# Three stages of a fused block in one program block, with the token lists written during the middle one

## The reference

```python
x = x + xattn(_layernorm(x), ctx)      # q, k, v, o with LoRA; 257 context rows and the own 32 keys
x = x + rwkv_moe(_layernorm(x), ...)   # below
x = x + ffn(_layernorm(x), ...)        # shared GEGLU + one of 8 experts by argmax

# rwkv_moe
xn = _ln(x, ln1_g, ln1_b); xx = _shift(xn)
k, v, r = xk @ Wk, xv @ Wv, sigmoid(xr @ Wr)     # xk = xn*mu + xx*(1-mu), and so on
wkv = scan over the positions of exp-weighted sums of v
x = x + r * wkv @ Wo
ei = _ln(x, ln2_g, ln2_b); exx = _shift(ei)
probs = softmax(ei @ router_w); vals, idx = top_k(probs, 2)
k_e = square(relu(xk_e @ eWk[e])); r_e = sigmoid(xr_e @ eWr[e])
moe = sum over the two experts of weight * r_e * (k_e @ eWv[e])
return x + moe
```

## Time and profile before

| | us |
|---|---|
| median of three runs | 1025.69 (1024.75 to 1028.22) |
| the profiled execution | 1025.3 |
| its span, first to last instruction | 1023.6 |
| DVE in 157 to 304 (time mixing) | 120.5 of 147 busy |
| PE in 304 to 348 (routing) | 3.2 of 44 busy |
| PE in 348 to 542 (first experts) | 191.4 of 194 busy |

### The profile page before, as it was taken

How to read it: one execution, slowest core, us unless ns; L and a number is a source line. 1 busy time by engine, 2 the same in 40 slices (tenths; PEclk the granted TensorE clock), 3 DMA queues, 4 the chain that set the end, 5 groups by cost and what they waited for, 6 DMA issues and landing times. The chain is left out here.

```text
span 1023.6 us, 19906 instructions
## 1 busy us (share of the span) xinstructions
PE 893.4 (87%) x6694; PEld 809.5 (79%) x6695; DVE 438.7 (43%) x1126; ACT 291.2 (28%) x648; POOL 279.8 (27%) x520
## 2 busy tenths in 40 slices
PE   6899987889850499999995999995899999999995
PEld 4566657888840399999994999995799999999994
DVE  2354445999956455555552333335211111111113
ACT  1333324666620254554441111110011111111110
POOL 1664442444443232232203222220210010010006
PEclk8999998999965599999997999997999999999998
DMA  9887828511110242222212111010588988899715
GB/s 348 290 291 276 303 83 285 147 42 32 33 39 4 93 161 86 80 79 87 77 51 63 32 42 37 31 31 27 196 315 331 321 300 327 305 317 326 276 58 164
DMA packets 97918, 163.40 MB, mean 160 GB/s; under 512 B 10136, under 2 KB 76184, under 8 KB 95672
## 3 DMA queue, kind: packets, MB, share of 16 engines
q1 hardware_dynamic: 85552, 120.84, 34.4%
q0 software_dynamic: 6528, 19.54, 7.0%
q10 hardware_dynamic: 5776, 22.22, 5.4%
HBM read 146.06 MB, written 16.52 MB: 159 GB/s over the span
## 5 line engine op out<-in xcount | busy, mean ns | idle before, releaser
L1306 PEld LDWEIGHTS bank<-zT_f,we 128*128 128x128 f32 x1472 | 167.8, 192 | 3.3 <-issue 1.5
L1306 PE MATMUL bank<-zT_f,we 128*128 128x128 f32 x1472 | 168.3, 275 | 1.6 <-issue 1.1
L1323 DVE TENSOR_TENSOR hT_f<-bank,act_g 128x512 f32<-128x512 f32 x78 | 53.8, 691 | 230.4 <-PE bank L1306 217.1
L1315 ACT ACTIVATE act_g<-bank 128x512 f32<-128x512 f32 x78 | 46.6, 597 | 323.7 <-PE bank L1306 323.7
L1306 PE MATMUL bank<-zT_c,a_x 128*128 128x128 f32 x1024 | 122.7, 283 | 0.3 <-PEq L978 0.3
L1306 PEld LDWEIGHTS bank<-zT_c,a_x 128*128 128x128 f32 x1024 | 120.5, 199 | 0.8 <-issue 0.7
L726 PE MATMUL bank<-xn,mixed_w 128*128 128x128 f32 x768 | 94.0, 280 | 1.3 <-ACT xn L808 0.9
L726 PEld LDWEIGHTS bank<-xn,mixed_w 128*128 128x128 f32 x768 | 90.0, 195 | 2.3 <-ACT xn L808 1.3
L1330 PE MATMUL bank<-we,hT_f 128*128 128x256 f32 x368 | 83.3, 380 | 0.0
L1183 PE MATMUL bank<-xk,wk_e 128*128 128x128 f32 x624 | 78.0, 280 | 0.2
L1183 PEld LDWEIGHTS bank<-xk,wk_e 128*128 128x128 f32 x624 | 74.5, 196 | 0.9 <-DVE xr L1237 0.5
(11 more groups left out here) (227 smaller groups left out, 1286.7 us busy)
## 6 DMA issues: line engine op xcount, KB each, us to landing
we<-in_W_dram SPq DMA_DIRECT2D x69, 1024.0 KB, 7.3
ctx_sb<-in_ctx_n_dram ACTq DMA_DIRECT2D x16, 1152.0 KB, 7.4
kT<-in_ctx_t_dram SPq DMA_DIRECT2D x16, 1028.0 KB, 8.9
rows_y<-y SPq DMA_DIRECT2D x39, 128.0 KB, 1.7
ewk_sb<-in_eWk_dram SPq DMA_DIRECT2D x1, 4096.0 KB, 14.2
ewv_sb<-in_eWv_dram SPq DMA_DIRECT2D x1, 4096.0 KB
rows_f<-yr ACTq DMA_DIRECT2D x23, 128.0 KB, 6.2
ewr_sb<-in_eWr_dram SPq DMA_DIRECT2D x1, 2048.0 KB, 19.8
```

Of the source, the lines that this page charges most:

```text
L1306: last = nc.tensor.matmul(bank[half][:, f * P:(f + 1) * P], w12[:, i, k, col0:col0 + P], zT[:, k], start=k == 0, stop=k == KD - 1)
L1315: nc.scalar.activation(act_g[:, half], bU[half][:], ACT.Gelu).then_inc(self.ac_g, 1)
L1323: nc.vector.tensor_tensor(hT[:, parity, half * HH:(half + 1) * HH].rearrange("p f t -> p (f t)"), bG[half][:], act_g[:, half], ALU.mult).t ...
```

## The change

Attention, time mixing and first experts become one block; the routing block between them is gone. The semaphores of all three are cleared once, behind the experts.

- **Joint.** Each engine's list has attention steps 15, 16, 17 alternating with steps 0, 1, 2 of time mixing (`MIX_AT`), then steps 3 to 21. Buffers of the stages share two arenas; the expert weights are loaded when the last `x1` is written (`dv_x1`).
- **Step of time mixing.** DVE no longer adds the logits; for chunk s-5 it finds the two best experts (`largest`, `largest_at`), the one-hot rows, their sum (`mask`), the rank of the token in the expert and a row of a list (`listed`). The sum of weights goes to PSUM (`bB`), `key_rise` is one instruction. PE adds the router's bias by a product and makes the ranks by two products (`ranks`); ACT copies the logits (`router`). POOL orders its pairs by semaphores in place of drains, adds the mask to the running count (`count`), and last in its step, for chunk s-6, writes the token numbers to `tab_e` in DRAM by two indirect stores of 128 single elements (`list_tokens`).
- **Behind the last chunk** DVE makes the map of the 39 tiles (`tile_map`). SP then reads, for each tile, the place of its list from SBUF and loads 128 token numbers (`load_pick`), nine tiles ahead. POOL's loop over the tiles is written out: mix factors, gather, and for 16 tiles a piece of the addition of `a_x2` to `x1`.
- The mix factors `cm_mu` come with another load.

The core of the diff:

```diff
-            nc.clear_and_free_semaphores(att_sems)
-            nc.all_engine_barrier()
...
-            nc.clear_and_free_semaphores(mix_sems)
-            nc.all_engine_barrier()
...
-        routing("r1_", 2, NT1, logits, True, table1, expert1, slot1, gate, add_x2)
...
+        MIX_AT = G - 1
+        ATT_STEPS = G + 2
+        MIX_STEPS = G + 6
...
+            @block.vector
+            def _(dve):
+                att, mix = att_vector(dve), mix_vector(dve)
+                for s in range(ATT_STEPS):
+                    att(s)
+                    if s >= MIX_AT:
+                        mix(s - MIX_AT)
+                for s in range(ATT_STEPS - MIX_AT, MIX_STEPS):
+                    mix(s)
+                moe_vector(dve)
...
+            def list_tokens(n):
+                if n == 0:
+                    pool.wait_ge(zero_tab_out, 16)
+                pool.wait_ge(dv_slot, n + 1)
+                for k in range(2):
+                    nc.gpsimd.indirect_dma_start(out=tab_e[:, :],
+                                                 out_offset=bass.IndirectOffsetOnAxis(ap=listed[:, n, k:k + 1], axis=0),
+                                                 in_=token[:, n:n + 1], in_offset=None).then_inc(po_tab, 16)
...
+            def ranks(n):
+                pe.wait_ge(dv_mask, n + 1)
...
+                nc.tensor.matmul(bX[:, D:D + E], before_m[:], mask[:, n % 2], start=True, stop=False)
+                nc.tensor.matmul(bX[:, D:D + E], ones_m[:], earlier[:, n % 2], start=False, stop=True).then_inc(pe_rank, 1)
...
+            def largest(n):
+                dve.wait_ge(ac_lg, n + 1)
+                nc.vector.max(top[:, n], logits[:, n])
...
+        def moe_sync(sp):
+            def load_pick(n):
+                at = sp.value_load(place1[0:1, n:n + 1], min_val=0, max_val=T_ROWS // P - 1)
+                sp.dma_start(pick[:, n], tab_e[bass.ds(at * P, P), :]).then_inc(picked_by(n)[0], 16)
+            sp.wait_ge(dv_map, 1)
+            sp.wait_ge(po_tab, 2 * G * 16)
...
+            for n in range(NT1):
+                e = pool.value_load(expert1[0:1, n:n + 1], min_val=0, max_val=E - 1)
+                need(pool, m_dx, n - NM + 1)
+                pool.wait_ge(*picked_by(n))
+                nc.gpsimd.tensor_copy(mu_e[:, n % NM], cm_mu[:, :, e]).then_inc(m_mu, 1)
+                nc.gpsimd.indirect_dma_start(out=pair[:, n % NM], out_offset=None, in_=rows_e[:, :],
+                                             in_offset=bass.IndirectOffsetOnAxis(ap=pick[:, n], axis=0)
+                                             ).then_inc(m_got[n % NM], 16)
```

More of the change, by code:

```diff
@@ L163, in perceiver_block @@
         g1, b1, wd, u_c, g2_c, b2_c = (late[:, 22 + 2 * i:24 + 2 * i] for i in range(6))
-        g2, b2 = (late[:, 36 + D * i:36 + D * (i + 1)] for i in range(2))
+        cm_mu = late[:, 34:34 + 2 * E * KD].rearrange("p (i e k) -> p i e k", i=2, k=KD)
+        g2, b2 = (late[:, 66 + D * i:66 + D * (i + 1)] for i in range(2))
         wexp = sb("wexp", [P, KD])
@@ new lines, in perceiver_block @@
+        logits = sb("logits", [P, G, E])
+        top = sb("top", [P, G, 8])
+        top_at = sb("top_at", [P, 2, 8], U32)
+        hot = sb("hot", [P, G, 2, E])
+        listed = sb("listed", [P, G, 2], U32)
+        moved = sb("moved", [P, E])
+        moved_k = sb("moved_k", [P, G, 2])
+        mask = sb("mask", [P, 2, E], BF16)
+        earlier = sb("earlier", [P, 2, E], BF16)
+        hot_rank = sb("hot_rank", [P, 2, E])
+        rank = sb("rank", [P, 2])
+        token = sb("token", [P, G], I32)
@@ new lines, in perceiver_block @@
+        N3 = 3
+        in_a = Carve(arena_a, FLOATS_A)
+        w_T = in_a.take(4, KD, D)
+        early = in_a.take(EARLY)
+        bq_c, bk_c = early[:, 0:KD], early[:, KD:2 * KD]
+        bv_b, bo_b = early[:, 4:4 + D], early[:, 4 + D:4 + 2 * D]
+        ctx_sb = in_a.take(N3, BG * TC * D + D)
+        kT = [in_a.take(BG, KD, KW) for _ in range(N3)]
+        hn, v_own, o_nat = (in_a.take(2, D) for _ in range(3))
+        hnT, qT, oT = (in_a.take(2, KD, P) for _ in range(3))
+        prob = in_a.take(2, KW)
@@ new lines, in perceiver_block @@
+        probT = in_a.take(2, 3, P)
+        lora_sb = Carve(arena_b, FLOATS_B).take(8, D)[0:R]
+        in_b = Carve(arena_b, FLOATS_B)
+        z_in = in_b.take(2, D)
+        xn = [in_b.take(KD, BG, SP1) for _ in range(2)]
+        pp, dk, e1b, e2b, e_in, evb, num, den, rw = (in_b.take(2, D) for _ in range(9))
+        aa = in_b.take(2, D)
+        z3, ei = in_b.take(2, D), in_b.take(2, D)
+        zT3 = in_b.take(2, KD, P)
+        NM = 3
+        in_a = Carve(arena_a, FLOATS_A)
+        ewk_sb = in_a.take(E, KD * FK)
@@ new lines, in perceiver_block @@
+        ewv_sb = in_a.take(E, FKC * D)
+        ewr_sb = in_a.take(E, KD * D)
+        in_b = Carve(arena_b, FLOATS_B)
+        cmp_eg = in_b.take(E, G)
+        cmp_te = in_b.take(NT1, E)
+        hot_moved = in_a.take(G * 2, E)
+        in_b = Carve(arena_b, FLOATS_B)
+        pair = in_b.take(NM, 2 * D)
+        wk_e = in_b.take(NM, KD * FK)
+        prevT, diffT, xk, xr = (in_b.take(NM, KD * P) for _ in range(4))
+        sig, y = in_b.take(NM, D), in_b.take(NM, D)
+        h_relu = sb("h_relu", [P, NM, FK], F32, moe_scope)
```

1801 lines of the change are left out of this document (959 added, 842 removed).

## The result

The changed kernel took 1036.82 us, median of four (1032.66 to 1041.92), beside 1025.22 us for the kernel before (four, 1024.2 to 1028.22): ratio 1.0111, 95% interval 1.0056 to 1.0165, slower by some 11 us where 21 less were forecast. Its profiled execution took 1038.94 us, span 1037.2, mean clock of TensorE 0.938 (before 1025.3, 1023.6 and 0.943).

A forecast was written before the change was run, and what follows sets the result against it. DVE was taken to bound time mixing, serial routing to follow, and PE the first experts. First transposes 21.9 us earlier (joint, steps and tail together) and +1.0 for a clear took 1025.3 to 1004.4, said as 1004.5; range 991 to 1015.

The forecast's parts named there:

- step 5 begins: DVE's step 5 of time mixing, after the joint with attention: begins at 187.9, before 189.73.
- twelve steps: Time mixing, DVE steps 5 to 17: 8.4 us each in place of 8.12, plus 3.4 us.
- step 17 to the first tile: Tail from DVE's step 17 to PE's first transposes: 37.1 us in place of 60.6, minus 23.5.
- first tile to the next stage's first gather: First experts: tile work hidden under PE; one new semaphore clear with its barrier, plus 1.0 us.
- X: Start of step 17, forecast at 288.7; last list store issued at X + 26.3, PE starts at X + 37.1.
- The step of 8.4: Time-mixing step: path 8.3, POOL without slack, 0.1 added for SBUF meetings; bounds 8.0 to 8.9 us.
- 8.1 for DVE by itself: DVE's own work in a time-mixing step: loses 0.75 us, gains 0.8, so even at 8.1.
- the path through the logits: In time mixing, `largest` waits for ACT's logits copy: 9.15 plus DVE's 7.5, 16.65 us for two steps.
- A: Rival: time-mixing steps do not lengthen, 8.0 us each, 4.8 less: 999.6 us; chance 0.2.
- B: Rival: list stores dearer on POOL, 1.55 each; step 8.9, +6.0, tail's four pairs +2.3: 1012.8 us; chance 0.15.
- C: Rival: POOL's list stores wait for DVE; a pair costs 6.0, step 10.4: 1028.4 us; chance 0.05.
- The joint: Attention to time mixing: 1.5 us earlier, DVE's step 2 at 165.2 against 166.71.

The follow-up runs named there:

- entries of 64 bytes: Changed kernel with list entries in `tab_e` of 64 bytes in place of 4, row stores unchanged: 1000.81 us, ratio 0.978.
- 16 and 15 rows: Changed kernel with each 31-row store to `rows_e` cut into 16 and 15 rows, lists unchanged: 1007.90 us, ratio 0.9837.

## Why the prediction was wrong

Against its own terms, in the profiled executions (us):

| term | forecast | change | entries of 64 bytes |
|---|---|---|---|
| step 5 begins | 187.9 | 190.57 | 188.93 |
| twelve steps | 100.8 | 117.5 | 102.1 |
| step 17 to the first tile | 37.1 | 50.9 | 33.1 |
| first tile to the next stage's first gather (before 197.2) | +1.0 | +1.15 | +1.1 |
| from there to the end (before 478.6) | 0 | +1.3 | -2.9 |

The sum of the change's misses, 2.7 + 16.7 + 13.8 + 0.15 + 1.3, is 34.6 us, from 1004.4 to 1039.0 (measured 1038.9).

**The step that failed** is one assumption in two terms. "The `rows_e` stores, which took 5.8 us to land, end near X + 27 and hide", and "For the landing of a store I have only gathers as bound from above ... I take 3.3". For the same reason the 8.4 us of a step hold no wait for `rows_e` at all, where POOL waited for it 11 times, 30.1 us in all. I took the row stores' landing as fixed and priced the list stores as work on POOL alone. That a transfer that I add can slow one that is there was in none of my cases, and its trace was at hand: two buffers are two steps, 16.2 us, of which 5.8 of landing leave some 10 of room; but a stream of 25 GB/s through one engine fills most of each step, and no room helps once it takes more than a step. In the tail the failed value appears twice: POOL's last store is 7.1 us later than forecast (X + 33.4 for X + 26.3), for waits on `rows_e`, and it takes 9.8 us to land, not 3.3 (352.46 less SP's 1.25, less 341.41). That is 13.6 of 13.8 us.

**The step of 8.4 was right as a number, by luck.** Without list stores, with 16 and 15 rows, and with 64-byte entries the steps are 8.43 us in the middle of the stage. The forecast had 8.1 for DVE by itself, and came to 8.4 by the path through the logits and a POOL without slack. With 64-byte entries neither binds: between 197.1 and 289 DVE waits for no other engine, its `max` included, so its own list takes 8.43. POOL waits 1.0 us a step for the moments and 1.3 for DVE's part of the numerator. DVE's sum was 0.3 too low, and the path and POOL were charged what they didn't cost. Only at 8.68 us is the forecast path seen, with 0.36 us of wait of `max` for ACT's logits in nine steps. A list store takes 1.08 and 0.96 us of POOL with 0.30 between, 2.3 a pair where 2.5 was forecast. Rivals A and B are out with that, and C too: POOL's stores did not wait for DVE. C's 1028.4 lies nearest to the 1036.8 measured, but for a reason that isn't there. B's tail of +2.3 was itself too small: four pairs at its price of 0.58 more a store are 4.6.

**The joint came near its size, by two misses that cancel.** In the changed kernel's profiled execution attention itself ran some 2 us late: TensorE's clock was granted at 0.70 in 20 to 40 us, 0.83 before, and attention's first residual came at 42.8 in place of 40.7. Counted from that residual, step 5 begins after 147.7 us, 149.0 before: 1.3 us earlier, where 1.8 was forecast. But the last residual of attention, counted the same way, came 1.8 us later than forecast. ACT's last copy of attention stands behind the exponents and gate of chunk 0, at 164.81, and DVE waited 5 us for the projection behind it:

```profile
166.41 0.48 DVE L630 SCALAR_TENSOR_TENSOR x<-bank,srec,xz 128x256 f32<-128x256 f32 x1 [5.17 <-PE bank L501]
```

I had listed that copy with 0.8 us "behind its gate", as if the gate were done. Steps 2 to 4 took 21.5 us where 22.7 was forecast, and that made up for most of it. Nor is it the lacing that gains: without it, step 5 comes 147.3 us after attention's first residual, with it 146.8 (both with 16 and 15 rows). With the lacing one step later and 64-byte entries it comes after 144.0, in place of 147.8. What sets the rhythm of 8.43 or of 8.68 us was not tried; at 8.68 POOL's third small operation takes 0.66 us in place of 0.40.

**Experts and what lies behind** came out as said: one clear more, +1.1 us, and tiles bound by PE. The 2.9 us that the last stages gained with 64-byte entries I didn't follow up.

With 64-byte entries the time is 1000.8 where 1004.5 was forecast. The terms don't agree as well as the time does: step 5 is 1.0 late, the steps 1.3 longer, the tail 4.0 shorter (the last store issued 2.5 earlier, its landing 1.4 quicker), and the last stages 2.9 shorter. The last store landed in 1.9 us (318.04 less 1.25 less 314.88), where 3.3 was forecast; over all 32 list stores the median from issue to landing is 3.5. The Trainium skill, DMA: Bandwidth & Descriptors, section on the anatomy of a DMA on the SWDGE path, has some 2.0 us fixed for such a transfer. The last store's 1.9 us agrees with that; the 9.8 us of the changed kernel is 8 us off.

Shown: that list stores cause the loss; that in the steps it needs both their 4-byte words side by side and the row stores of 31 rows; and that in the tail the words side by side are enough. Between 4 and 32 bytes no distance was run. Not shown: at what place in the memory or the engine such words wait. The run with words side by side in partition order has it as well as the changed kernel, where neighbours in an expert come from any partition, so nothing here says whether the writers must be different engines. 32-byte entries hold up no row store here, and 4-byte words 544 bytes apart cost 3 us with all of POOL's work for them, so width alone doesn't decide. The Trainium skill, DMA: Bandwidth & Descriptors, Specifications, says that below 512 bytes a DMA engine reads, changes and writes back. If that alone made the wait, both of these would wait as well.

## What to carry to other kernels

When a change adds transfers, look at what already runs through few DMA engines: a store of 31 rows moved at 25 GB/s here, and what held up that stream held up the buffer behind it. Scattered 4-byte words that the partitions of a store put side by side in memory were dear, 9.8 us to land at the end of the stage and a brake on their neighbours; give each its own 32 or 64 bytes, which gave this kernel 32 and 36 us. And behind indirect stores, link POOL's dependent operations with semaphores; a drain there cost 3 to 5 us. Last, read a right number by its terms: the 8.4 us of a step were forecast from a path and an engine that didn't bind.

## What the runs showed of the hardware that I had not expected

- 4-byte words of one store side by side: 40 us over 32 stores against 4-byte words 544 bytes apart (1067.5 and 1027.6 us), with the same instructions.
- A drain on POOL behind two indirect stores takes 3.1 to 4.5 us, for 4, 64 and 512 bytes a partition alike.
- SP's issue of four 31-row transfers took up to 18.9 us beside list stores with words side by side, and with four `ei` buffers, in place of 1.5; SP issues nothing else meanwhile.
- With 64-byte entries the last indirect store has landed 1.9 us after its issue, where a gather takes 3.4 us; the median of all 32 is 3.5.
